# Cross-attention stage of a decoder block: the reciprocal root of the layer norm goes to GpSimd, both bias additions to VectorE, and the row transposes one step later

## The reference, cut to what matters

```
x   = x + softmax(mask(q k^T)) v W_o + b_o     # 8 heads of 64, 224 queries, 750 keys
xn  = (x - mean) / sqrt(var + 1e-5)            # layer norm: what the experts read
s   = softmax(xn @ w_router); top 2 of 8 experts, slots in order of arrival
out = x + bias                                 # the experts' outputs are added to it later
```

## Time and profile before

| | |
|---|---|
| median of three runs | 3285.65 us (3281.9 to 3287.87) |
| the profiled execution's own time | 3286.76 us |
| its span | 3284.9 us |
| TensorE busy in the span | 3043.6 us (93%) |
| VectorE busy | 1644.6 us (50%) |
| ScalarE busy | 1347.1 us (41%) |
| GpSimd busy | 733.1 us (22%) |
| `normalise`, VectorE L1200, 112x750, 256 of them | 609 ns least, 611 median, 2781 greatest |

### The profile page before, as it was taken

The page is one execution under the profiler, slowest core; times in us unless marked ns, Lnnn a source line. Parts: engine busy times, 40 slices in busy tenths (PEclk is TensorE's granted clock), DMA queues, the critical chain, the costliest instruction groups (busy, mean ns, idle before and its releaser), DMA issues. The chain is left out here.

```text
span 3284.9 us, 50660 instructions
## 1 busy us (share of the span) xinstructions
PE 3043.6 (93%) x19312; PEld 2491.3 (76%) x19312; DVE 1644.6 (50%) x3785; ACT 1347.1 (41%) x2298; POOL 733.1 (22%) x560
## 2 busy tenths in 40 slices
PE   6889999878999999999999959999999999999997
PEld 4667777756777777777777738888888888888886
DVE  5888888863555556555555633323233323333321
ACT  5677777764555555555555521111111111121111
POOL 0000000011112122221212124242524242424232
PEclk9889999989999999999999969999999999999999
DMA  2011111124111111111111013141414141414132
GB/s 98 23 35 46 44 37 42 45 80 132 39 38 38 44 37 51 54 37 37 38 43 37 17 48 102 52 97 52 97 52 104 51 102 52 97 52 97 52 74 36
DMA packets 93874, 189.70 MB, mean 58 GB/s; under 512 B 17568, under 2 KB 27552, under 8 KB 91712
## 3 DMA queue, kind: packets, MB, share of 16 engines
q1 hardware_dynamic: 79168, 158.68, 15.9%
q0 software_dynamic: 14592, 29.43, 5.0%
HBM read 140.25 MB, written 47.82 MB: 57 GB/s over the span
## 5 line engine op out<-in xcount | busy, mean ns | idle before, releaser
L1757 ACT ACTIVATE f_hf<-f_h 128x448 f32<-128x448 f32 x256 | 139.8, 546 | 1012.4 <-PE f_h L1784 979.7
L1728 DVE CAST f_hh<-f_hf 128x448 fp32r<-128x448 f32 x256 | 106.4, 416 | 845.3 <-ACT f_hf L1757 824.5
L1799 PE MATMUL f_y<-f_w2h,f_hh 128*128 128x512 f32 x896 | 357.4, 399 | 0.0
L1687 POOL TENSOR_TENSOR f_w1l<-f_raw,f_w1h 128x512 fp32r<-128x512 f32 x128 | 182.4, 1425 | 777.3 <-DVE f_w1h L1711 777.1
L1799 PE MATMUL f_y<-f_w2h,f_hl 128*128 128x512 f32 x896 | 354.0, 395 | 0.0
L1799 PE MATMUL f_y<-f_w2l,f_hh 128*128 128x512 f32 x896 | 352.2, 393 | 0.0
L1380 ACT ACTIVATE c_s_sb<-c_s_sb,c_nmx 112x750 f32<-112x750 f32 x256 | 236.1, 922 | 200.4 <-DVE c_nmx L1214 198.5
L1372 ACT COPY c_pT<-psum 125x672 f32<-125x672 f32 x256 | 184.8, 722 | 244.8 <-PE psum L1475 236.8
L1475 PEld LDWEIGHTS psum<-a_ident,c_s_sb 112*125 112x125 f32 x1536 | 199.2, 195 | 93.7 <-issue 88.8
L1784 PE MATMUL f_h<-f_xTh,f_w1h 128*128 128x448 f32 x1024 | 254.8, 370 | 2.9 <-DVE f_xTl L1716 1.4
L1784 PE MATMUL f_h<-f_xTl,f_w1h 128*128 128x448 f32 x1024 | 250.0, 366 | 0.0
(11 more groups left out here) (246 smaller groups left out, 5833.5 us busy)
## 6 DMA issues: line engine op xcount, KB each, us to landing
f_raw<-in_w SPq DMA_DIRECT2D x128, 512.0 KB, 4.2
h_craw<-in_ctxT SPq DMA_DIRECT2D x16, 1125.0 KB, 5.1
a_x_in<-in_x SPq DMA_DIRECT2D x9, 896.0 KB, 5.7
a_xr<-in_x SPq DMA_DIRECT2D x8, 896.0 KB, 6.0
x_dram<-a_xr SPq DMA_DIRECT2D x8, 896.0 KB, 4.8
q_dram<-a_q SPq DMA_DIRECT2D x32, 224.0 KB, 5.6
h_q<-q_dram SPq DMA_DIRECT2D x16, 448.0 KB, 5.4
c_x<-x_dram SPq DMA_DIRECT2D x16, 448.0 KB, 4.9
```

The costliest lines, as they stand in the source:

```text
L1687: pool.tensor_tensor(w1s[1][:, l % NSLOT].rearrange("p k c -> p (k c)"), raw1[:, g % 2, l % 2, :], w1s[0][:, l % NSLOT].rearrange("p k c - ...
L1728: dve.tensor_copy(hs[0][:, l % 2, c * HC:c * HC + HC], hf[:, c, :]).then_inc(h_hi, 1)
L1757: act.activation(hf[:, c, :], H[:, 0:HC], ACT.Gelu_apprx_tanh).then_inc(free, 1)
L1799: mm = pe.matmul(Y[t][:], hs[a][:, l % 2, 128 * t:128 * t + 128], w2s[b][:, l % NSLOT, :], start=j == 0 and q == 0, stop=last_of_expert(l) ...
```

## The change: the root on GpSimd, the additions on VectorE, XT in steps 8 and 9

- `layernorm` is gone from VectorE. In step 6 GpSimd waits for both variances and makes the reciprocal root with 12 instructions: an initial guess in one instruction instead of two, one third-order step and one Newton step. Behind each it waits for the one before and increments a semaphore that nobody waits for (`newton_seen`).
- VectorE makes the two `xn` halves in the tail of step 7, behind the masking of head 9.
- `xo` is made by VectorE in the tail of step 9, `x1 + b_o` in the tail of step 13. The first `x1 + b_o`, ahead of the loop, stays on GpSimd.
- `XT(0)` goes from step 7 to step 8, slot 2. `XT(1)` goes from step 8, slot 2, to step 9, slot 1, ahead of `PV(1)`. Each now waits for its own half of `xn`. The order of the banks changes with that: before it was K(0,1), XT(0), K(1,0), XT(1), PV(1); now it is K(0,1), K(1,0), XT(0), XT(1), PV(1).
- ScalarE evacuates both in step 9: `XT(0)` behind K(1,0) and ahead of the copy of head 8, `XT(1)` behind the exponential of head 11.

```diff
-            4: ([], [OUT(1)], []), 5: ([], [PV(0)], []), 6: ([], [K(0, 0)], []), 7: ([], [K(0, 1)], [XT(0)]),
-            8: ([], [K(1, 0)], [XT(1)]), 9: ([], [PV(1)], []), 10: ([], [V(0, 0)], [RT]), 11: ([K(1, 1)], [K(2, 0)], []),
+            4: ([], [OUT(1)], []), 5: ([], [PV(0)], []), 6: ([], [K(0, 0)], []), 7: ([], [K(0, 1)], []),
+            8: ([], [K(1, 0)], [XT(0)]), 9: ([], [XT(1), PV(1)], []), 10: ([], [V(0, 0)], [RT]), 11: ([K(1, 1)], [K(2, 0)], []),
...
+        def root_of_variance(i):
+            var, square, product = nt[:, 0, :], nt[:, 1, :], nt[:, 2, :]
+            done = [0]
+            def then(ins):
+                done[0] += 1
+                ins.then_inc(newton, 1)
+                pool.wait_ge(newton, i * NEWTON - NEWTON + done[0])
+                pool.sem_inc(newton_seen, 1)
+            wait_apart(pool, mv_made, i * 2)
+            pool.sem_inc(newton_seen, 1)
+            then(pool.tensor_scalar(var, mv[:, :, 1], LN_EPS, None, ALU.add))
+            then(pool.tensor_scalar(rstd[:].bitcast(I32), var.bitcast(I32), -0.5, float(0x5f3759df), ALU.mult, ALU.add))
+            then(pool.tensor_tensor(square, rstd[:], rstd[:], ALU.mult))
+            then(pool.tensor_tensor(product, square, var, ALU.mult))
+            then(pool.tensor_scalar(square, product, -10 / 3, None, ALU.add))
+            then(pool.tensor_tensor(square, square, product, ALU.mult))
+            then(pool.tensor_scalar(square, square, 5.0, 3 / 8, ALU.add, ALU.mult))
+            then(pool.tensor_tensor(rstd[:], square, rstd[:], ALU.mult))
...
+            pool.sem_inc(rstd_made, 1)
         def tail(i, kind, s):
-            if s == 9:
-                wait_apart(pool, xn_made, i * 2)
-                pool.wait_ge(out_stored, i * 16 - 16)
-                pool.tensor_tensor(xo[:], x1[:], bi[:, None, :].broadcast_to([R, 2, C]), ALU.add).then_inc(xo_made, 1)
-            if s == 14 and kind != "end":
-                add_bias(i)
+            if s == 6:
+                root_of_variance(i)
...
# VectorE
+        def rows_with_bias(i):
+            wait_apart(dve, out_stored, i * 16 - 16)
+            dve.tensor_tensor(xo[:], x1[:], bi[:, None, :].broadcast_to([R, 2, C]), ALU.add).then_inc(xo_made, 1)
+        def add_bias(i):
+            wait_apart(dve, x_loaded, i * 16 + 16)
+            dve.tensor_tensor(x1[:], x1[:], bo[:, None, :].broadcast_to([R, 2, C]), ALU.add).then_inc(x1b_made, 1)
         def tail(i, kind, s):
+            if s == 9:
+                rows_with_bias(i)
+            elif s == 13 and kind != "end":
+                add_bias(i)
...
-            elif s == 6:
-                layernorm(i)
+            elif s == 7:
+                rows_normalised(i)
# ScalarE
+                if s == 9 and kind != "first":
+                    evacuate(i, kind, XT(0))
...
+                if s == 9 and kind != "first":
+                    evacuate(i, kind, XT(1))
# TensorE
-                if m == 0:
-                    pe.wait_ge(xn_made, i * 2)
+                pe.wait_ge(xn_made, i * 2 - 1 + m)
```

More of the change, by code:

```diff
@@ L937, in cross_attention @@
     ROUTE = 21
-    NEWTON = 13
+    NEWTON = 12
     psum, gen = handover.psum, handover.gen
@@ L978, in projections @@
     def projections(kind, s, slots):
-        return [u for u in units(kind, s, slots) if u[0] in ("K", "V", "XT")]
+        return [u for u in units(kind, s, slots) if u[0] in ("K", "V")]
     def number(lists, i, kind, unit):
@@ L1039, in cross_attention @@
     mv_made, root_made, rstd_made, xn_made = (sem(n) for n in ("mv_made", "root_made", "rstd_made", "xn_made"))
-    newton = sem("newton")
+    newton, newton_seen = sem("newton"), sem("newton_seen")
     lg_made, le_made, route, sel_made, slots_made, sent = (sem(n) for n in ("lg_made", "le_made", "route", "sel_made", "slots_made", "sent"))
@@ L1152, in add_bias @@
             pool.tensor_tensor(x1[:], x1[:], bo[:, None, :].broadcast_to([R, 2, C]), ALU.add).then_inc(x1b_made, 1)
-        def tail(i, kind, s):
-            if s == 9:
-                wait_apart(pool, xn_made, i * 2)
-                pool.wait_ge(out_stored, i * 16 - 16)
-                pool.tensor_tensor(xo[:], x1[:], bi[:, None, :].broadcast_to([R, 2, C]), ALU.add).then_inc(xo_made, 1)
-            if s == 14 and kind != "end":
-                add_bias(i)
+        def root_of_variance(i):
[16 more added lines that the diff above has]
+            then(pool.tensor_tensor(rstd[:], square, rstd[:], ALU.mult))
+            then(pool.tensor_tensor(square, rstd[:], rstd[:], ALU.mult))
+            then(pool.tensor_tensor(product, square, var, ALU.mult))
+            then(pool.tensor_scalar(product, product, -0.5, 1.5, ALU.mult, ALU.add))
+            then(pool.tensor_tensor(rstd[:], product, rstd[:], ALU.mult))
+            assert done[0] == NEWTON
+            pool.sem_inc(rstd_made, 1)
+        def tail(i, kind, s):
+            if s == 6:
+                root_of_variance(i)
             if s != 15:
@@ L1229, in residual, with rows_normalised @@
             dve.bn_aggr(mv[:, j, :], stats[:, j, :]).then_inc(mv_made, 1)
[L1231 to L1252, removed]
+        def rows_normalised(i):
             dve.wait_ge(xn_stored, i * 16 - 16)
@@ L1383, in tail @@
         def tail(i, kind, s):
-            if kind == "end" and s in (7, 8):
-                evacuate(i, kind, XT(s - 7))
-            elif s == 11:
+            if s == 11:
                 act.wait_ge(gen_free[BANK[kind, RT]], uses_before(i, kind, RT) + 1)
@@ L1434, in _ @@
                 hi_of_outputs(B - 1, "end", NM - 1)
+            elif s == 9:
+                evacuate(B, "end", XT(0))
+                evacuate(B, "end", XT(1))
             tail(B, "end", s)
```

## The result

The changed kernel takes 3231.66 us (median of 4, 3229.13 to 3237.46). The kernel before took 3285.55 on the same chip (median of 4). The ratio is 0.984, with a 95% interval from 0.9828 to 0.9853, so it is 54 us faster. The forecast was 34.5 us faster, 3252, and 3241 was the low end of its range: the sign was right, the size was not. The profiled execution took 3229.13 us with a span of 3227.3.

A forecast was written before the change was run, and what follows sets the result against it. TensorE was taken as the bound, 77.0 of 80 us busy. Holes -24.5, clock -8.5, `last` -4 and `end` +2.5 made -34.5 us from 3286.76, given as 3252; range 3241 to 3271, to hold 8 in 10.

The forecast's parts named there:

- TensorE's holes in steps 7 to 9: TensorE's idle stretches of 1.24 ahead of XT(0), 0.91 ahead of the scores and 0.39 ahead of PV(1): 2.54 us an iteration.
- The scores' wait: TensorE ahead of the scores of heads 10 and 11: about 0.2 us left of the holes of 1.24 and 0.91.
- the new wait at XT(1): TensorE at XT(1) waits about 0.5 us for ScalarE's copy of K(1,0), whose bank it now takes.
- the root: Reciprocal root on GpSimd: 12 instructions at 0.45 us, 5.4 us in all, ready before VectorE comes to xn.
- the conditions under which I said I was wrong: In the new profile: xn waits for the root, the clock drops stay, or the period is above 70 us.
- Holes: TensorE, 14 middle iterations: 1.75 us gained in each, bounds 1.3 and 2.3; 24.5 us in all.
- The third of the old holes: TensorE ahead of PV(1): 0.39 us of waiting for ScalarE's copy of K(1,0), counted in the 2.54 an iteration.
- Clock: Middle iterations: 7 of 9 clock drops of 1.2 us go, 8.5 us gained; bounds 11 gained to 6 lost.
- Rival 1: Clock drops stay because the wait at XT(1) stands among light transposes: 3261, with 5 more drops 3267; chance 0.16.
- `last`: Last iteration, bound by VectorE's chain: loses root, xn and a scaling's blocked 2.17 us; 4 us gained (2 to 5).
- `end`: Final pass, where nothing hides the root: 5.4 us on GpSimd against 2.85 on VectorE, 2.5 us lost.
- GpSimd loses 5 us of long additions, which nobody waited for in the middle: Bias additions moved to VectorE, into its waits in steps 10 and 14: cost 0, at worst 0.1 us each.

The follow-up runs named there:

- the first pair: The kernel before and the changed kernel, first measured on the same chip: 3285.55 and 3231.66 us, ratio 0.984.
- the second experiment: The kernel before with only the two bias additions moved from GpSimd to VectorE: 3269.31 us, ratio 0.9991.

## Why the prediction was right and where it was wrong

**Right.** TensorE's holes in steps 7 to 9 were the place. The scores' wait was put at 0.2 (0.19), the new wait at XT(1) at 0.5 (0.38), PV(1) at 5.9 behind the scores (5.88), the root at 5.4 us (4.9), held by scalings for about the 0.6 expected (two instructions, 0.17 and 0.37). The experiments bear the parts out one by one: root on VectorE +22 us, `xn` ahead of the masking +26, XT as before +10, a root that is 1.49 late +0.97 an iteration. They don't add up to the gain: each is what the part is worth once all the others are there. Of the conditions under which I said I was wrong, none came about.

**The mis-sized terms.**
- Holes: I took 1.75 us an iteration and measured 1.97, 27.6 instead of 24.5. My own balance of TensorE gave 1.74 with a wait of 0.5 and 0.1 at PV(1) and 0.1 for the scaling; they were 0.38, 0 and 0. The bounds (1.3 to 2.3) held it. The third of the old holes, 0.39 ahead of PV(1), stands in only 6 of the 14 iterations, mostly those without a clock drop (in its two repeats 10 and 4); as the price of a drop is taken from whole periods, the account by periods still closes.
- Clock: 7 of 9 drops were to go, all 9 went, 10.8 instead of 8.5; again inside its bounds. Rival 1 was wrong: the holes of 0.19 and 0.38 brought no drop in 14 iterations.
- `last` 4.8 instead of 4, `end` -0.7 instead of -2.5. Of the latter -1.6 is the root, which is shorter than I put it.

These make 42.5 us, 3244: inside the range, 8 below the forecast. What put the result below 3241 is two terms that the sum did not have. The first alone is enough for the medians (10 us less, 3234); the second belongs to the two profiled executions.
- **The level at which the profile of before was taken.** This is the step that failed: I counted TensorE's holes in steps 7 to 9 alone and put ScalarE's wait at its loop's edge at nothing, without looking. Of the 10 us that are left in the middle iterations it is 8.5, and the long clock drop is 1.3. The kernel before paid for the wait at every edge but one: the 70.63 of the earlier trace rows, which I took as the undisturbed period, holds 0.65 of it, and the same program with the short wait has 70.0. So I forecast a period of 68.9 and it is 68.05, 0.65 of the difference from the edge and 0.2 from the holes. It moves by job: 3272 to 3286 for the kernel before, 3232 to 3238 for the kernel after. Where both had the short wait, the change is worth 40 us; where both had the long one in most iterations, 46 to 47, and there the kernel before had 12 clock drops instead of 6. That it goes with the job was shown by the repeats. Why the kernel after had the shorter wait in the first pair, and so how much of the 54 us is the change's own, and what ScalarE does in that time, I have not tested; it stays open.
- **Chance ahead of the stage.** At 815 us, where nothing is changed, the kernel before is already 5.8 us behind. Its time at 1.2 GHz up to there is 129.7 us against 119.5; the other twelve profiles lie between 126.3 and 136.5 whatever the kernel, and reach the same product between 810.5 and 815.5 us, the kernel after at 808.5. Its profiled execution was also the fastest of its four, 2.5 us under the median. The range had nothing for that.

**The step that was right as a sum and wrong as a reason.** "GpSimd loses 5 us of long additions, which nobody waited for in the middle" priced the additions' move at nothing. That holds for the kernel before alone (3.5 us in the second experiment, hardly clear of nothing). Beside the other parts it is worth the whole gain, 43.6 us: behind the later `xn`, GpSimd's addition would meet a scaling in every iteration. I had the row for it, 2.78 beside 2.35, and used it for the root and for `last` alone. The Trainium skill's rule in "SBUF — State Buffer", "Who interferes with whom", that the engine which issues second waits for a whole instruction of the first, agrees with the 2.41 us of the scaling behind an addition of 2.38 that began 0.38 before it.

## What to carry to other kernels

When an operation on GpSimd is released by one that you move, work out what it will run beside at its new place; here 2.4 us of GpSimd just ahead of VectorE's scaling held it for 1.8 us, and right behind a scaling they cost nothing. A change that closes TensorE's holes is worth more than the holes where they bring clock drops, so price each drop and give the range room for all of them to go. Read the waits of the whole iteration, the loop's edge too, before calling a period undisturbed. Before explaining a difference below half a per cent, run both kernels in a second job: here one kernel moved by 14 us from job to job while the other moved by 7.

## What was not expected of the hardware

- A dependent chain of tiny instructions on GpSimd (112x2, each behind a wait for the one before, with an extra semaphore increment) runs at 0.375 us from start to start, 0.19 of it busy. On VectorE the same kind of chain took 2.85 us for 13, 0.22 each.
- ScalarE's wait at the edge of its loop takes one of a few values, about 0.39 (only the wait for the transposes), 0.75, 1.46 or 2.15 us; two jobs showed 0.39 throughout, the others mixtures. No run changed it on purpose.
- TensorE's clock fell behind single holes of 2.17 us in 12 of 14 iterations, 1.84 in 8, 1.76 in 1, and 1.35 or less in none; behind the pair 1.24 and 0.91 with one product between them in 6, 7, 9 and 12 of 14 in four profiles. A fall of 3.4 us cost 1.0 to 1.8 us of the period; two falls lasted 6.8 us and cost 2.5.
